# A fused attention and quantised feed-forward kernel: signed gate integers on GpSimd, and forty gate units finished in the up pass

## The reference, cut to what matters

```
def act_qdq(x):
    qmax = 2.0 ** (ACT_BITS - 1) - 1.0
    scale = jnp.maximum(jnp.max(jnp.abs(x)) / qmax, 1e-12)
    return jnp.clip(jnp.round(x / scale), -qmax - 1.0, qmax) * scale
...
x = act_qdq(x)
up = act_qdq(x @ lpbq_dequant(w_up).T)
gate = act_qdq(x @ lpbq_dequant(w_gate).T)
sig = fixed_qdq_u16(jax.nn.sigmoid(gate))
gate = act_qdq(gate * sig)
o = act_qdq(gate * up)
return o @ lpbq_dequant(w_down).T
```

## Time and profile before

| what | us |
|---|---|
| median of three timed runs (2347.78 to 2349.55) | 2347.9 |
| span of the profiled execution | 2347.3 |
| opening and attention, until the first matmul of the gate pass | 646.9 |
| gate and up pass, one piece of TensorE's work | 996.9 |
| no matmul: the end of the gate's work, the stage of the last peak, the first integers of o | 193.1 |
| down pass, one piece of TensorE's work | 497.6 |

### The profile page before, as it was taken

How to read it: one execution, slowest core, us unless ns; L and a number is a source line. 1 busy time by engine, 2 the same in 40 slices (tenths; PEclk the granted TensorE clock), 3 DMA queues, 4 the chain that set the end, 5 groups by cost and what they waited for, 6 DMA issues and landing times.

```text
span 2347.3 us, 25386 instructions
## 1 busy us (share of the span) xinstructions
PE 2020.4 (86%) x9524; PEld 945.0 (40%) x9524; DVE 1715.7 (73%) x1387; ACT 1398.2 (60%) x1599; POOL 670.6 (29%) x662
## 2 busy tenths in 40 slices
PE   5888888888599999999999999999000699999998
PEld 2444444444244444444444444444000344444443
DVE  8799999999634534532499998999899644577641
ACT  4678887887422322322499996676899633366530
POOL 2599999998300000000121110222111000000000
PEclk9999999999799999999999999999555899999999
DMA  7789999998346656743699995787998755555541
GB/s 297 283 314 337 348 337 346 335 350 316 126 181 226 225 207 223 259 148 144 242 378 390 378 369 209 264 320 293 401 419 327 291 229 208 205 201 232 233 152 72
DMA packets 131162, 634.60 MB, mean 270 GB/s; under 512 B 12256, under 2 KB 12768, under 8 KB 91104
## 3 DMA queue, kind: packets, MB, share of 16 engines
q1 hardware_dynamic: 85888, 316.81, 37.0%
q0 software_dynamic: 45152, 316.16, 34.6%
HBM read 430.69 MB, written 202.24 MB: 270 GB/s over the span
## 4 chain that ended last, share of the span: by engine, by line
PE 64%; issue 3%; DVE 3%; ACT 2%; POOL 0%; DVEq 0%; ACTq 0%; POOLq 0%
PE fd_pp L1777 42%; PE fd_pp L1791 21%; ACT ff_ring L1720 1%; DVE ff_sig L1575 1%; DVE ff_h_parts L1559 1%; DVE ff_sq L1497 1%; ACT ff_sig L1707 0%; DVE ff_sq L1566 0%; DVE kept_gate L1568 0%; DVE ff_gin L1510 0%; DVE ff_hq L1549 0%; ACT ff_hq L1632 0%; ACT ff_ring L1746 0%; ACT ff_sig L1736 0%; DVE kept_o_peak L1575 0%
## 5 line engine op out<-in xcount | busy, mean ns | idle before, releaser
L1791 PE MATMUL fd_pp<-ff_down,kept_gate 128*128 128x512 f16 x1536 | 458.9, 381 | 193.1 <-DVE ff_up L1616 193.1
L1777 PE MATMUL fd_pp<-ff_h_parts,kept_gate 128*128 128x512 f16 x2304 | 499.6, 380 | 14.3 <-DVE ff_h_parts L1415 14.3
L1777 PE MATMUL fd_pp<-ff_h_parts,ff_up 128*128 128x512 f16 x2304 | 497.4, 379 | 0.0
L1639 ACT ACTIVATE ff_raw<-fd_pp 128x1024 f32<-128x1024 f32 x192 | 194.3, 1017 | 396.5 <-PE fd_pp L1777 396.5
L1777 PEld LDWEIGHTS fd_pp<-ff_h_parts,kept_gate 128*128 128x128 f16 x2304 | 225.9, 98 | 287.9 <-DVE ff_h_parts L1415 14.7
L1777 PEld LDWEIGHTS fd_pp<-ff_h_parts,ff_up 128*128 128x128 f16 x2304 | 225.4, 98 | 271.8
L1420 DVE TENSOR_REDUCE kept_gate_peak<-ff_raw 128x1 f32<-128x2048 f32 x48 | 109.7, 2285 | 292.9 <-ACT ff_raw L1639 292.9
L1791 PEld LDWEIGHTS fd_pp<-ff_down,kept_gate 128*128 128x128 f16 x1536 | 150.6, 98 | 375.9 <-issue 195.8
L1791 PE MATMUL fd_pp<-ff_down,ff_up 128*128 128x512 f16 x768 | 292.2, 380 | 0.0
L1746 ACT ACTIVATE ff_ring<-ff_hq,kept_g 128x2048 int16<-128x2048 f32 x48 | 96.0, 1999 | 191.1 <-DVE ff_hq L1549 189.7
L790 PE MATMUL at_psO<-kept_wo,at_ahi 128*128 128x512 f16 x512 | 155.5, 386 | 36.2 <-ACT at_alo L277 31.6
(11 more groups left out here) (239 smaller groups left out, 3454.9 us busy)
## 6 DMA issues: line engine op xcount, KB each, us to landing
ff_raw<-up_scratch SPq DMA_DIRECT2D x66, 1024.0 KB, 8.5
gate_scratch<-ff_raw POOLq DMA_DIRECT2D x48, 1024.0 KB, 9.1
ff_gin<-gate_scratch SPq DMA_DIRECT2D x48, 1024.0 KB, 8.7
up_scratch<-ff_raw POOLq DMA_DIRECT2D x48, 1024.0 KB, 7.7
ff_gin<-gate_integers SPq DMA_DIRECT2D x73, 512.0 KB, 5.8
gate_integers<-ff_ring POOLq DMA_DIRECT2D x43, 512.0 KB, 8.7
ff_up<-up_scratch SPq DMA_DIRECT2D x21, 1024.0 KB, 9.5
kept_xs<-in_x SPq DMA_DIRECT2D x32, 512.0 KB, 14.6
```

What stands on the lines that cost most here:

```text
L1639: nc.scalar.activation(raw[:, n % UNITS, h * 2 * BLK:(h + 1) * 2 * BLK], pp[(2 * n + h) % 4][:, :, :].rearrange("p a t -> p (a t)"), ACT.C ...
L1777: mm = nc.tensor.matmul(pp[k % 4][:, h, :], wt[w][:, c, f:f + P], a[:, b % 2, :, c, :], start=(q == 0), stop=(q == len(todo) - 1))
L1791: mm = nc.tensor.matmul(pp[k % 8 // 2][:, k % 2, :], a[b % 2][:, f, t * P:(t + 1) * P], wt[w][:, f, :], start=(q == 0 and i == 0), stop=(q ...
```

## The change

The magnitudes of the gate integers (`ab`) are no longer formed in the up pass's first part. DVE multiplies the signed integers by `sq` with a factor -1 and keeps the greatest, which gives the peak over negative gates; for positive gates the greatest product belongs to the greatest gate, so the gate pass keeps also the greatest signed value of each unit (`gate_top`, one more DVE reduction per unit), and one column takes it through integer, sigmoid, sigmoid integer and product (`greatest_gated`). All 48 units' integers are formed by POOL, one iteration ahead, behind `store_raw` in its queue. READY goes from 36 to 40 (SECOND from 30 to 28), KEPT from 8 to 10, with two units kept where `ab` was, and WQ from 4 to 2.

```diff
-READY = 36
+READY = 40
-KEPT = 8
+KEPT = 10
...
-    WQ, NEAR = 4, 7
+    WQ, NEAR = 2, 7
...
-            return spare[:, j, :] if j < 6 else more[:, j - 6, :]
+            return spare[:, j, :] if j < 6 else more[:, j - 6, :] if j < 8 else ab[:, j - 8, :]
...
                         else:
                             have_gq(sp, u - GR)
-                            sp.wait_ge(m["ab"], u - GR + 1)
...
+                def gate_integers(u):
+                    pool.wait_ge(gate_in[u % GR], 16 * (u // GR + 1))
+                    gq_free(pool, u)
+                    if u >= AWAY:
+                        pool.wait_ge(m["mm"], NB * PAIRS)
+                    nc.gpsimd.tensor_scalar(integers(u), gin[:, u % GR, :], g[:, 5:6], 1.0, ALU.mult, ALU.mult).then_inc(m["gq"], 1)
...
                     if n >= 1:
                         store_raw(NU + n - 1)
+                    for u in first_units(n + 1):
+                        gate_integers(u)
                     for v in second_units(n - 1):
                         store_gated(v)
...
                     to, k = ("gate_peak", n) if n < NU else ("up_peak", n - NU)
+                    if n < NU:
+                        nc.vector.tensor_reduce(keep["gate_top"][:, n:n + 1], raw[:, n % UNITS, :], AX.X, ALU.max)
                     nc.vector.tensor_reduce(keep[to][:, k:k + 1], raw[:, n % UNITS, :], AX.X, ALU.max,
                                             apply_absolute_value=True).then_inc(m["peak"], 1)
...
-                gpk_v(dve)
+                nc.vector.tensor_reduce(g_red[:, 0:1], keep["gate_peak"][:, :], AX.X, ALU.max)
+                nc.vector.tensor_reduce(g_red[:, 1:2], keep["gate_top"][:, :], AX.X, ALU.max).then_inc(m["g_red"], 1)
...
+                nc.vector.tensor_scalar(top_i[:, :], g_all[:, 1:2], g[:, 5:6], None, ALU.mult).then_inc(m["top"], 1)
+
+                def greatest_gated():
+                    dve.wait_ge(m["top_s"], 1)
+                    nc.vector.tensor_scalar(top_q[:, :], top_s[:, :], 65536.0, 65535.0, ALU.mult, ALU.min).then_inc(m["top_q"], 1)
+                    dve.wait_ge(m["top_q"], 1)
+                    link(nc.vector.tensor_tensor(keep["gated_peak"][:, NU:NU + 1], top_i[:, :], top_q[:, :], ALU.mult))
...
                 def first(u):
                     sigmoid_integer(u, u % 2)
-                    gate_integers(u + 2)
-                    dve.wait_ge(m["ab"], u + 1)
-                    nc.vector.tensor_tensor_reduce(out=sig[:, u % 2, :], in0=ab[:, u % 2, :], in1=sq[:, :], scale=1.0,
+                    nc.vector.tensor_tensor_reduce(out=sig[:, u % 2, :], in0=integers(u), in1=sq[:, :], scale=-1.0,
...
                 def first(u):
-                    act.wait_ge(gate_in[u % GR], 16 * (u // GR + 1))
-                    if u % 3 == 0:
-                        gq_free(act, u)
-                        if u >= AWAY:
-                            act.wait_ge(m["mm"], NB * PAIRS)
-                        nc.scalar.activation(integers(u), gin[:, u % GR, :], ACT.Copy, scale=g[:, 5:6]).then_inc(m["gq_act"], 1)
                     need(act, m["gpeak"], u - 1)
-                    nc.scalar.activation(ab[:, u % 2, :], gin[:, u % GR, :], ACT.Abs, scale=g[:, 5:6]).then_inc(m["ab"], 1)
                     have_gq(act, u)
                     nc.scalar.activation(sig[:, u % 2, :], integers(u), ACT.Sigmoid, scale=g[:, 4:5]).then_inc(m["sig"], 1)
```

More of the change, by code:

```diff
@@ L920, in feed_memory @@
            "h_parts": s.sb("h_parts", [P, 2, 2, SUB, DC, P], F16), "raw": s.sb("raw", [P, UNITS, UE], F32)}
-    for n in ("red_w", "all_w", "unit_w", *(f"{a}_{b}" for a in "gpuo" for b in ("red", "all"))):
+    for n in ("red_w", "all_w", "unit_w", *(f"{a}_{b}" for a in "puo" for b in ("red", "all"))):
         mem[n] = s.sb(n, [P, 1], F32)
+    for n in ("g_red", "g_all"):
+        mem[n] = s.sb(n, [P, 2], F32)
+    mem["top_i"], mem["top_s"], mem["top_q"] = (s.sb(n, [P, 1], dt) for n, dt in (("top_i", I16), ("top_s", F32), ("top_q", U16)))
     return mem
@@ L1059, in feed @@
                    "hq ah al mm out peak w_peak w_red w_all w_scales w_sent w_q w_real w_hi w_lo "
-                   "gq_act gq_dve ab sig sq gpeak g2 mag gp neg ga_late ga_act ga_dve ua prod "
+                   "gq sig sq gpeak top top_s top_q g2 mag gp neg ga_late ga_act ga_dve ua prod "
                    "fsig fsq fgp fgq fuq fo foq foh fol fmm y")
-        gpk, gpk_v, gpk_p = whole_peak(nc, mem, m, "g", keep["gate_peak"][:, :])
+        g_red, g_all, top_i, top_s, top_q = (mem[n] for n in ("g_red", "g_all", "top_i", "top_s", "top_q"))
         ppk, ppk_v, ppk_p = whole_peak(nc, mem, m, "p", keep["gated_peak"][:, :])
@@ L1107, in have_gq @@
         def have_gq(eng, u):
-            if u % 3 == 0:
-                eng.wait_ge(m["gq_act"], u // 3 + 1)
-            else:
-                eng.wait_ge(m["gq_dve"], u - u // 3)
+            eng.wait_ge(m["gq"], u + 1)
         def gq_free(eng, u):
@@ L1117, in gq_free @@
                 eng.wait_ge(gq_out[u % QR], 16 * (u // QR))
-                eng.wait_ge(m["sig"], u - QR + 1)
+                eng.wait_ge(m["gpeak"], u - QR + 1)
         def sig_free(eng, k):
@@ L1142, in gated @@
             if kind == "wq":
-                return hq[:, j, :] if j < 2 else ab[:, j - 2, :]
+                return hq[:, j, :]
             return again(j - AWAY if j >= AWAY else j + KEPT)
@@ L1228, in load_again @@
                         if w < AR:
-                            sp.wait_ge(m["sig"], NU)
-                            sp.wait_ge(m["ab"], NU)
+                            sp.wait_ge(m["gq"], NU)
+                            sp.wait_ge(m["gpeak"], NU)
                             for r in range(QR):
@@ L1369, in _ @@
                         nc.gpsimd.partition_all_reduce(allm[:, :], red[:, :], P, PEAK).then_inc(m["w_all"], 1)
-                gpk_p(pool)
+                pool.wait_ge(m["g_red"], 1)
+                nc.gpsimd.partition_all_reduce(g_all[:, :], g_red[:, :], P, PEAK).then_inc(m["g_all"], 1)
+                pool.wait_ge(m["g_scales"], 1)
+                pool.wait_ge(m["w_lo"], 2 * PIECES)
+                for u in first_units(0):
+                    gate_integers(u)
                 for n in range(NU):
@@ L1477, in _ @@
                 dve.wait_ge(m["peak"], NU)
-                gpk_v(dve)
+                nc.vector.tensor_reduce(g_red[:, 0:1], keep["gate_peak"][:, :], AX.X, ALU.max)
+                nc.vector.tensor_reduce(g_red[:, 1:2], keep["gate_top"][:, :], AX.X, ALU.max).then_inc(m["g_red"], 1)
                 link(nc.vector.tensor_tensor(g[:, 3:4], g[:, 0:1], al_[:, 5:6], ALU.mult))
                 dve.wait_ge(m["g_all"], 1)
-                quantiser(nc, link, g[:, 4:5], g[:, 5:6], gpk[:, :], g[:, 2:3])
+                quantiser(nc, link, g[:, 4:5], g[:, 5:6], g_all[:, 0:1], g[:, 2:3])
                 nc.vector.tensor_scalar(g[:, 6:7], g[:, 4:5], 1.0 / 65536.0, None, ALU.mult).then_inc(m["g_scales"], 1)
@@ L1484, in _ @@
                 dve.wait_ge(m["w_lo"], 2 * PIECES)
[L1486 to L1489, removed]
-                        if u >= AWAY:
-                            dve.wait_ge(m["mm"], NB * PAIRS)
-                        nc.vector.tensor_scalar(integers(u), gin[:, u % GR, :], g[:, 5:6], None, ALU.mult).then_inc(m["gq_dve"], 1)
+                nc.vector.tensor_scalar(top_i[:, :], g_all[:, 1:2], g[:, 5:6], None, ALU.mult).then_inc(m["top"], 1)
[4 more added lines that the diff above has]
+                    link(nc.vector.tensor_tensor(keep["gated_peak"][:, NU:NU + 1], top_i[:, :], top_q[:, :], ALU.mult))
                 def sigmoid_integer(k, a):
@@ L1511, in second @@
                                                    op0=ALU.mult, op1=ALU.mult).then_inc(m["g2"], 1)
-                gate_integers(1)
                 for n in range(NU):
+                    if n == 2:
+                        greatest_gated()
                     if n % UNITS == 1 and n // UNITS + 1 < NB:
@@ L1686, in _ @@
                 for n in range(NU):
+                    if n == 1:
+                        act.wait_ge(m["top"], 1)
+                        nc.scalar.activation(top_s[:, :], top_i[:, :], ACT.Sigmoid, scale=g[:, 4:5]).then_inc(m["top_s"], 1)
                     for u in first_units(n)[:1]:
@@ L1816, in build @@
             "h_peak": s.sb("h_peak", [P, NT // 2], F32), "gate_peak": s.sb("gate_peak", [P, U3], F32),
-            "up_peak": s.sb("up_peak", [P, U3], F32), "gated_peak": s.sb("gated_peak", [P, U3], F32),
+            "up_peak": s.sb("up_peak", [P, U3], F32), "gated_peak": s.sb("gated_peak", [P, U3 + 1], F32),
+            "gate_top": s.sb("gate_top", [P, U3], F32),
             "o_peak": s.sb("o_peak", [P, U3], F32),
```

## The result

The kernel after takes **2439.3 us** (median of four runs, 2437.5 to 2442.5) against 2347.8 for the kernel before (four runs): a ratio of 1.039, 95% interval 1.038 to 1.041. The forecast was 2433.

A forecast was written before the change was run, and what follows sets the result against it. Bound: TensorE's unbroken matmul passes, with the last peak's stage on ACT and DVE between them. 2347.9 + 2.5 + 64.5 + 30 - 12 gave 2433 us; the range for 8 in 10 was 2358 to 2499.

The forecast's parts named there:

- Gate pass: Gate pass: second DVE reduction per unit hidden for 47 of 48; the last and a small one cost +2.5 us.
- First part: Up pass until the first part's last product: 48 POOL passes of 2.37 us outweigh DVE's 41.1 us saved; +64.5 us.
- the mechanism named: Up pass, first part: POOL's passes and DVE's sigmoid integers and products exclude each other, so DVE sets TensorE's pace.
- 8.2 us of DVE's idle time: Up pass, first part: idle time in which POOL can work, taken off the part's length.
- Second part: Rest of the up pass: four more finished units, 14.3 us, and late h loads, less DVE's idle 20.9; +30 us.
- The h loads: Up pass, second part: loads for blocks 12 to 15 stand behind a reload awaiting a later store; 4 x 9.1 = 36.4 us.
- Last stage: Last peak's stage: 12 late units become 8, relieving ACT and DVE; -12 us, between -14 and 0 if DMA limits.
- A: Up pass, first part: POOL's pass costs 4.74 us like its two-input rows, +113.7, giving 2547 us; chance 0.15.
- B: Up pass: POOL's passes cost DVE nothing, first part at TensorE's pace, only h loads late; 2363 us; chance 0.14.
- C: Up pass: POOL's passes fit beside reductions and h loads land in time; only last stage moves; 2336 us; chance 0.06.

The follow-up runs named there:

- experiment 1: Kernel after with each load of a block's h integers issued two iterations earlier in SP's queue: 2402.1 us, 1.023 times before.
- experiment 5: Kernel before with the h loads of the last four blocks issued one iteration later: 2370.7 us, ratio 1.010.
- experiment 6: Kernel after with READY back at 36 and KEPT at 8: 2410.7 us, 1.027 times before.
- experiment 2: Kernel after with the 48 integer passes on ScalarE instead of GpSimd, h loads still late: 2369.8 us, 1.009 times before.
- experiment 3: Kernel after with the integers on ScalarE and the h loads two iterations earlier: 2341.6 us, 0.997 times before.
- experiment 7: Kernel after with GpSimd's pass replaced by a memset that writes a constant and reads nothing: 2371.9 us, 1.010 times before.
- experiment 8: Kernel after with integers on ScalarE, h loads two iterations earlier and READY 42 instead of 40: 2340.3 us, 0.9965 times before.
- experiment 4: Kernel after with each of GpSimd's 48 integer passes done twice into the same place: 2490.5 us, 1.061 times before.

## Why the prediction was right, step by step

**Gate pass, +2.5:** +2.2. The second reduction is hidden for all units but the last.

**First part, +64.5:** +57.7, by the mechanism named. Three terms were of another size.
- GpSimd's pass was put at 2.37 us; it takes 1.97. 48 are 94.6 us instead of 113.8. The nearest row was ACT's 1.99, which the prediction named and left for half the rate of a two-input addition. The estimate of 1.76 that the prediction had from the Trainium skill (GPSIMD Engine Reference, 3.1) is too short by 0.2.
- Nearly all of that is paid by DVE: from the groups, products +54.8 us, the split's subtractions +32.3, sigmoid integers +3.5, together 90.6. The prediction counted on the sigmoid integer and the product. But only one of the 48 sigmoid integers met a pass, the first of all; the others kept their 1.22. And it overlooked the subtraction, which has two inputs in SBUF as well. Since passes were summed, not meetings, the sum did not suffer; that something kept out stood beside nearly every pass was in the queue's order, but which operation it was came out otherwise.
- The prediction let GpSimd work in 8.2 us of DVE's idle time. DVE's idle time grew instead, from 10.2 to 15.4 us (the stretch less DVE's busy time in its window), 11.1 of it ahead of the first sigmoid integer (6.0 before): GpSimd begins its first pass only 7.0 us after its all-reduce, as the next row of the kernel after shows.

```profile
1160.17 1.96 POOL L1340 TENSOR_SCALAR ff_ring<-ff_gin,kept_g 128x2048 int16<-128x2048 f32 x1 [7.00 <-issue]
```

-41.1 + 90.6 + 5.2 is 54.7; the last 3.0 us I can't place, except that neighbouring DVE operations overlap by some 0.08 us in the timeline, so that 32 removed ones gave back 2.6 us less than their durations. Against the forecast the shorter pass and the unpaid 4.0 us made 23 us less, and the idle time 13 us and these 3.0 more: that they partly cancel is luck.

**Second part, +30:** +36.1. The h loads cost 35.2 us in four waits (forecast 36.4), and experiments 1, 5 and 6 show the cause to be the one that was named. What was missing is mainly 5.9 us in which DVE waits for the all-reduce of the gated peak: GpSimd is idle for 8.78 us ahead of it, and no releaser is shown. A record of GpSimd's queue and the timeline of the kernel after:

```profile
L898 POOLq MODIFY_POOL_CONFIG  x2: 37/37/37, 1504.3 to 1504.3; - x2
...
1512.80 0.38 POOL L898 PARTITION_ALL_REDUCE ff_p_all<-ff_p_red  x1 [8.78 <-issue]
```

The same had stood in the trace of before, in the attention, where GpSimd goes from additions to an all-reduce:

```profile
635.33 0.38 POOL L732 PARTITION_ALL_REDUCE at_last_all<-kept_eps_d  x1 [6.12 <-issue]
```

The prediction had not read it. GpSimd's queue has the two MODIFY_POOL_CONFIG records at the start of each such gap: at 629.4 in the kernel before, and at 1153.1 and 1504.3 in the kernel after. The up pass of experiments 2, 3, 7 and 8, where GpSimd makes no such pass, has none, and DVE's wait is gone. The gap is 5.9 to 8.8 us each time GpSimd goes from one kind to the other, and the change puts 48 passes between two all-reduces, so it comes twice.

**Last stage, -12:** -7.7. The prediction had bounded this term at 0 for the case that the DMA engines are the next limit, and rows speak for some of that: in 1748 to 1835 of the kernel after the DMA share is 1.02 at 420 GB/s, as in the earlier trace rows, while ACT's busy time has gone from 82.3 to 78.1 of 87 us and DVE's from 81.4 to 77.5. The chain of the kernel before has no transfer in this stage; that of the kernel after has three loads of gate units, 23.3 us in all:

```profile
1764.78 8.41 DMA ff_sig<-gate_integers
...
1805.78 7.88 DMA ff_ab<-gate_integers
...
1891.18 6.99 DMA ff_sig<-gate_integers
```

So loads now help to set this stage's length. Whether they are late because the DMA engines are full or because there are two load slots fewer (WQ 2 for 4) is open: no run changed the transfers or WQ alone at 40 units. Taking two more units out (experiment 8) gave 1 us.

**Rivals.** A (4.74 us a pass) and B (no exclusion) fall by the rows of the pass and the product. C's mechanism, loads in time whatever the queue, falls by the four waits; with both costs taken out (experiment 3) the kernel takes 2341.6 us, near the 2336 which C gave for that case.

## What to carry to other kernels

Work moved to an idle GpSimd is free only beside DVE operations that it does not keep out: go through DVE's operations in the stretch where it will run, by what releases it, and, if the work reads SBUF, count every us beside a two-input one as lost, on DVE or on GpSimd. When a ring's depth or a count moves a wait to a later store, look for whatever else stands in the same queue behind that wait. Here ScalarE had the room (246 of 288 us), and with that and the loads moved up the same change is 0.26% faster than the kernel before instead of 3.9% slower.

## What the runs showed of the hardware

- Which DVE operations a GpSimd pass keeps out depends on what both do. A pass that reads and writes SBUF kept out the product (1.96 us longer for 1.97 of pass), the subtraction, the sigmoid integer and (in experiment 4, 3 us over two of them) the cast; one that only writes (memset, 1.82 us) kept out the sigmoid integer and not the product or the subtraction; neither touched the reduction. The Trainium skill (SBUF — State Buffer, Who interferes with whom) states both halves: two SBUF inputs collide with a GpSimd instruction that reads, not with one that only writes, and an operation in a two-port mode collides with GpSimd without that limit. The runs agree with the first half. That the sigmoid integer is in such a mode no row says; its 1.22 us against 2.29 for the product fits it.
- GpSimd's change between an all-reduce and a tensor pass: 7.0 us ahead of the first pass (5.9 of them after the scales stand), 8.8 ahead of the all-reduce after it, each with two MODIFY_POOL_CONFIG records at its start. The memset of experiment 7 began 1.15 us after its all-reduce, as soon as the scales stood, without such records. The Trainium skill (GPSIMD Engine Reference, 2.1) gives about 6 us for loading code on the first call to a freshly loaded kernel. The rows are of that size or longer, and show the gap again on the way back; that it is the loading of code no row says.
- TensorE's granted clock, 1.00 and 0.99 in the two parts of the up pass before, was 0.93 in the mean in 1154 to 1501 and in 1501 to 1746 after, where it pauses for DVE (1.00 is the upper level, 2.4 GHz, and the 0.50 of the earlier trace rows, where no matmul runs, the lower, 1.2 GHz). Its 2304 matmuls of the up pass were busy for 522.3 us, against 499.5 in the gate pass, but TensorE still stood 63.7 us for DVE there. DVE set the pace, and no row shows that the clock cost time.
